# Two multiplies of the chunk loop on another engine, and a reciprocal on the other side of a broadcast, in a linear-attention block

## The reference

```
xn   = layernorm(x)
q, k, v = silu(xn @ Wq), silu(xn @ Wk), silu(xn @ Wv)         # 16 heads of 64
for each chunk of 128 tokens, per head:
    scores = (q_i @ k_i^T) * mask                             # mask = exp(-s*(i-j)), lower triangle
    o_i    = scores @ v_i + lam_q * (q_i @ kv)
    kv     = lam_c * kv + (k_i * lam_k)^T @ v_i               # 64x64 state per head
o = (o - mean(o)) * rsqrt(var(o) + 1e-5) * gamma + beta
s = (o * sigmoid(xn @ Wg1 @ Wg2)) @ Wo
g = silu(xn @ (W + lora)^T + b)
y = x + s * g
```

## Time and profile before

| | |
|---|---|
| time, median of 3 runs | 746.3 us (746.19 to 748.85) |
| profiled execution, its own time | 746.53 us |
| its span, slowest core (core 6) | 744.8 us |
| spans of the 8 cores | 736.3 to 744.8 us |
| busy share of the span | PE 68%, DVE 40%, ACT 30%, POOL 12% |
| chunk loop, 300 to 448 us | 148 us, PE clock granted 0.65 of full speed |
| stage 4c, 554 to 745 us | 191 us, PE clock 0.76 to 738 us |

### The profile page before, as it was taken

One profiled execution on the slowest core, in us unless ns is written; L12 is line 12 of the kernel. 1 busy time (PEld: TensorE's weight loads), 2 busy tenths in 40 slices (PEclk: granted clock), 3 DMA queues, 4 the chain that ended last, 5 costly groups with the idle time before them and its releaser, 6 DMA issues.

```text
span 744.8 us, 8401 instructions; the slowest of 8 cores (736.3 to 744.8 us)
## 1 busy us (share of the span) xinstructions
PE 507.5 (68%) x2644; PEld 248.3 (33%) x2678; DVE 298.8 (40%) x627; ACT 226.4 (30%) x425; POOL 89.5 (12%) x76
## 2 busy tenths in 40 slices
PE   0118181999999993456666666899976686776773
PEld 0003131444444441234444443134433232333321
DVE  1350515121021001555555556410006777787784
ACT  1134434366333331133333331652331111111110
POOL 0000000000002000244454441000000000000000
PEclk9999586899999997575575576589995868787787
DMA  8771302000058995100000002230001223143243
GB/s 250 246 227 57 113 28 85 1 1 1 0 195 174 176 177 156 51 1 1 1 1 1 1 1 68 85 114 0 1 1 28 39 47 56 29 57 57 29 57 58
DMA packets 14049, 49.73 MB, mean 67 GB/s; under 512 B 3728, under 2 KB 3729, under 8 KB 13878
## 3 DMA queue, kind: packets, MB, share of 16 engines
q0 software_dynamic: 2448, 16.78, 14.1%
q1 hardware_dynamic: 9254, 24.02, 10.5%
q10 hardware_dynamic: 2304, 8.39, 3.6%
HBM read 40.79 MB, written 16.78 MB: 77 GB/s over the span
## 4 chain that ended last, share of the span: by engine, by line
PE 46%; DVE 18%; issue 9%; ACT 9%; DMA 8%; another core or an unknown queue 7%; DVEq 1%; SPq 1%; POOL 0%; ACTq 0%; POOLq 0%
PE pb L436 15%; PE pb L830 8%; PE pb L946 6%; DMA LANDB<-wq 3%; DVE SAB L613 2%; PE pb L662 2%; PE pb L817 2%; DVE RSROW L918 2%; PE pb L538 2%; PE pb L669 2%; PE pb L649 2%; PE pb L599 2%; DMA LUPF<-lup 2%; ACT VO L691 2%
## 5 line engine op out<-in xcount | busy, mean ns | idle before, releaser
L436 PE MATMUL pb<-XNT,WS 128*128 128x512 bf16 x500 | 117.7, 395 | 17.6 <-ACT XNT L495 16.9
L436 PEld LDWEIGHTS pb<-XNT,WS 128*128 128x128 bf16 x512 | 51.3, 101 | 81.7 <-issue 27.6
L649 PE MATMUL pb<-SAB,VO 128*128 128x256 bf16 x128 | 29.5, 346 | 58.4 <-DVE SAB L619 34.7
L489 PE MATMUL pb<-IDB,XNTM 128*128 128x128 bf16 x128 | 13.6, 271 | 72.5 <-DVE XNTM L478 48.4
L402 DVE CAST WS<-LAND 128x1024 bf16<-128x1024 f32 x20 | 14.6, 729 | 118.0 <-DMA LAND<-w 55.2
L830 PE MATMUL pb<-WS,XNT 128*128 128x512 bf16 x251 | 58.4, 383 | 0.5 <-issue 0.3
L685 ACT ACTIVATE VO<-pb 64x256 bf16<-64x256 f32 x64 | 24.2, 377 | 109.6 <-PE pb L669 106.6
L538 PE MATMUL pb<-WS,XNT 128*128 128x512 bf16 x251 | 55.3, 379 | 1.9 <-DVE WS L402 1.6
L675 POOL TENSOR_TENSOR KVBD<-KVBD,LAMCB 128x512 bf16<-128x512 bf16 x32 | 36.9, 1152 | 139.2 <-DVE KVBD L701 66.4
L946 PE MATMUL pb<-WS,CCo 128*128 128x512 bf16 x122 | 44.2, 512 | 3.2 <-DVE CCo L932 1.2
L958 POOL DMA_DIRECT2D y<-SGT x16 | 13.8, 865 | 269.8 <-DVE SGT L953 269.8
(11 more groups left out here) (100 smaller groups left out, 768.4 us busy)
## 6 DMA issues: line engine op xcount, KB each, us to landing
y<-SGT POOLq DMA_DIRECT2D x16, 512.0 KB, 5.6
XV<-x ACTq DMA_DIRECT2D x12, 512.0 KB, 13.3
XTS<-x ACTq DMA_DIRECT2D x4, 512.0 KB, 8.0
LAND<-wq SPq DMA_DIRECT2D x4, 512.0 KB, 6.1
LANDB<-wq SPq DMA_DIRECT2D x4, 512.0 KB, 6.4
LAND<-wk SPq DMA_DIRECT2D x4, 512.0 KB, 4.2
LANDB<-wk SPq DMA_DIRECT2D x4, 512.0 KB, 5.0
LAND<-wv SPq DMA_DIRECT2D x4, 512.0 KB, 3.9
```

Of the source, the lines that this page charges most:

```text
L436: p.pe(lambda e, k=k, oc=oc, t4=t4, bank=bank, wten=wten: e.matmul(PB[bank][:], wten[:, k * 1024 + oc * 128:k * 1024 + (oc + 1) * 128], XN ...
L489: p.pe(lambda e, f=f, xn=xn, bank=bank: e.matmul(pbh(bank)[:, f * 128:(f + 1) * 128], xn[:, f * 128:(f + 1) * 128], IDB[:], start=(f == 0) ...
L649: p.pe(lambda e, pp=pp, c=c, ob=ob, ocol=ocol, w=w, i=i: e.matmul(PB[ob][:, ocol:ocol + 256], VO[:, c * 1024 + pp * 128:c * 1024 + (pp + 1 ...
```

## The change

Three edits. In the chunk loop the multiply into QH (L638) and the decay of the state (L675) are issued to VectorE instead of GpSimd, at the same places of the program text, with the same operands. In stage 4c the square-root row itself is broadcast by the matmul, and VectorE takes the reciprocal of the broadcast 128x128 block out of PSUM into RBI in SBUF; the eight L926 read RBI in place of PSUM.

```diff
@@ -635,7 +635,7 @@
         qsrc = A(QT, 0, c * 128, [[2048, 8], [1, 128]])
         qdst = A(QH, 0, csl * 1024, [[128, 8], [1, 128]])
         lsrc = A(LAMQB, 0, 0, [[128, 8], [1, 128]])
-        p.pool(lambda e, qsrc=qsrc, qdst=qdst, lsrc=lsrc: e.tensor_tensor(
+        p.dve(lambda e, qsrc=qsrc, qdst=qdst, lsrc=lsrc: e.tensor_tensor(
             out=qdst, in0=qsrc, in1=lsrc, op=ALU.mult),
             reads=[bQT[pp][c // 4] for pp in range(8)] + [bLAMQ],
             writes=[bQH[csl]])
@@ -672,7 +672,7 @@
-            p.pool(lambda e, csl=csl, nsl=nsl, w=w: e.tensor_tensor(
+            p.dve(lambda e, csl=csl, nsl=nsl, w=w: e.tensor_tensor(
                 out=KVBD[:, nsl * 1024 + w * 512:nsl * 1024 + (w + 1) * 512],
                 in0=KVBD[:, csl * 1024 + w * 512:csl * 1024 + (w + 1) * 512],
                 in1=LAMCB[:, w * 512:(w + 1) * 512], op=ALU.mult),
@@ -915,20 +915,20 @@
             out=VROW[:], in_=PB[sb_st][0:1, 128:256],
             func=AF.Sqrt, scale=1.0 / E, bias=EPS),
             reads=[bPB[sb_st], bEPS], writes=[bROW])
-        p.dve(lambda e: e.reciprocal(out=RSROW[:], in_=VROW[:]),
-              reads=[bROW], writes=[bROW])
         p.pe(lambda e, sb_b=sb_b: e.matmul(
-            PB[sb_b][:, 128:256], ONESF[:], RSROW[:], start=True, stop=True),
+            PB[sb_b][:, 128:256], ONESF[:], VROW[:], start=True, stop=True),
             reads=[bONESF, bROW], writes=[bPB[sb_b]])
-
+        p.dve(lambda e, sb_b=sb_b: e.reciprocal(
+            out=RBI[:], in_=PB[sb_b][:, 128:256]),
+            reads=[bPB[sb_b]], writes=[bB128])
         for pp in range(8):
             bP = bCCP[par][pp]
-            p.dve(lambda e, CCt=CCt, pp=pp, sb_b=sb_b: e.scalar_tensor_tensor(
+            p.dve(lambda e, CCt=CCt, pp=pp: e.scalar_tensor_tensor(
                 out=CCt[:, pp * 128:(pp + 1) * 128],
                 in0=CCt[:, pp * 128:(pp + 1) * 128],
                 scalar=GAMB[:, pp * 128:pp * 128 + 1],
-                in1=PB[sb_b][:, 128:256], op0=ALU.mult, op1=ALU.mult),
-                reads=[bP, bPB[sb_b], bLAMC], writes=[bP])
+                in1=RBI[:], op0=ALU.mult, op1=ALU.mult),
+                reads=[bP, bB128, bLAMC], writes=[bP])
```

## The result

The changed kernel takes 773.3 us (median), the kernel before 746.7 in the runs beside it: a ratio of 1.0362, 95% interval 1.0346 to 1.0378, or 27 us slower (the medians differ by 26.6). The direction and the place were forecast, the size was not: 765.0 us, 18.3 us slower, with a range to 773.0.

What follows compares the result with a forecast made beforehand. The chunk loop was taken as bound by a ring of waits, with no engine full. Span 744.8 + 19.5 (QH) + 0 (decay) - 0.8 (reciprocal) = 763.5, 765.2 with 1.7 around the span, 765.0 as median; range 757 to 773 us.

Steps and rivals of the forecast that it cites:

- POOL's work was free: Chunk loop: GpSimd's QH and decay multiplies run about 3 us ahead of their readers, so removing them gains nothing.
- QH starts at T + 0.60, ends at T + 1.28, and L662 starts at T + 1.42: Chunk loop, half 0: QH queues behind L631 on VectorE, lasts 0.68 us, and L662 waits for it.
- T: Chunk loop: the start of L631 on VectorE in a chunk, from which the forecast counts its times.
- I take 1.3 us for each: 15 x 1.3 = 19.5 us: Chunk loop: delay from QH on VectorE in each of 15 chunks with an L662; ends 12.6 and 20.6 us.
- discount for chunks with a high clock: Chunk loop: in 8 of 15 chunks PE's clock was high before; delay there 0.84 us if it stays high.
- the ring: Chunk loop: cycle of waits, L696/L701, masks and L631 on DVE, PE matmuls, ACT copies; mean 9.03 us per chunk.
- The upper end, 20.6: Chunk loop: largest delay worked out for QH on VectorE, 7 x 1.27 + 8 x 1.47 us, all at low clock.
- Edit 2 at nothing: Chunk loop: state's decay (L675) on VectorE is covered in both halves and costs nothing; without cover half 0's costs 6 us.
- Edit 3 at -0.8 us: Stage 4c: reciprocal behind the broadcast keeps the 1.74 us path and gains in four tiles where L953 delayed it: -0.8 us.
- single-rate multiply: Rival, chunk loop: VectorE does strided QH at one element per cycle, 1.21 us, 8 us more: 773; chance 0.07.
- cheap L926: Rival, stage 4c: L926 gets shorter with an SBUF operand, 7.5 us go: 757.5; chance 0.06.
- high clock: Rival, chunk loop: PE's clock high throughout, chunk 8.95 us against 9.03, total 744.3, not slower; chance 0.04.

Runs made afterwards that it cites:

- The three single edits: Kernel before with one edit each, ratios to it: QH multiply on VectorE 1.0317, state's decay on VectorE 0.9999, reciprocal behind the broadcast 1.0027.
- QH in the gap: All three edits, but next chunk's QH issued on VectorE behind L701 of half 0, against the kernel before: ratio 1.0036, 749.9 us.
- one more swap: Kernel before with its chunk loop reordered, plus L669's state update issued first in each half: ratio 0.9280 to the kernel before, 693.1 us.
- reordered: Kernel before with scores, masks and transposes of chunk c+1 issued behind the halves of chunk c, same engines: ratio 0.9447, 707.3 us.

## Why the prediction was right and wrong

- *What bounds the loop, and that POOL's work was free:* right. The three single edits and QH in the gap show it: the loss is the place in VectorE's queue.
- *"QH starts at T + 0.60, ends at T + 1.28, and L662 starts at T + 1.42":* right to 0.01 us.
- *"I take 1.3 us for each: 15 x 1.3 = 19.5 us":* this step failed. It measured 23.7 us, 1.6 for each. L696 of half 0 came at T + 3.05 and not at T + 2.86 (L669 ends at 369.58, T + 2.88, and L696 follows 0.17 later), since 0.85 us is what L662 adds behind a running group, and behind a wait it takes 1.01: it has no predecessor to overlap, which costs 0.16 us. The row was there: L649 x4, after a wait, took 1.01 us in the earlier trace rows, and L662 x4 directly behind it 0.85. When the change put the wait in front of L662, its first matmul became the late one. And the discount for chunks with a high clock was wrong: the ring of the changed kernel is 3.77 + 3.05 + 3.89 = 10.71 us in the usual chunk, where before the mean was 9.08 and only the slowest chunks took 9.25. L662 of half 0 ran at the low clock from its start in 13 of the 15 chunks, in 6 of them although L649 in front of the wait had run at the high one, as in the chunk shown. 1.62 is so 1.27 (worked out) + 0.18 (lost overlap) + 0.17 (the fast chunks gone). The upper end, 20.6, had the clock but not the overlap.
- *Edit 2 at nothing:* right, 0.9999.
- *Edit 3 at -0.8 us:* wrong in sign, +2.0 us. The reciprocal (0.96) and L926 (+4 ns) were nearly as taken; "ACT to PE, about the same 0.14" was not (0.25), nor was the 0.10 in front of L926 (0.17). The matmul has two semaphores to wait for after the change: VectorE's, since the bank was last read by it, and ScalarE's. Before, the reciprocal's signal stood for both. From one L914 to the next the usual tile went from 10.99 to 11.22 us, more than the tails gave back; the mean went from 11.18 to 11.29, which makes 1.7 us in 15 tiles.
- *Rivals:* single-rate multiply, cheap L926 and high clock are each refuted by a row (682 ns, 344 ns, 0.57). By an estimate from the Trainium skill's figures (VectorE: DVE Perf Modes, the TRN2 errata) L926 would have become 65 ns shorter; the trace does not agree, it became 4 ns longer.
- *The total* ended 0.3 us above the range. Its sum had two terms too low, by 4.2 and 2.8 us. The worst case worked out for the first, 20.6, stood on the row of a group that had not waited, and the second had no bound for its hand-overs.

## What to carry to other kernels

Work on an idle helper engine is free as long as its lead covers it (3 us of lead for 2.12 us of work here); the faster engine is worth nothing if the instruction then stands behind others that wait for this iteration's data. Price a moved instruction by what stands ahead of it in the queue and by the state of what stands behind it: the group behind a new wait no longer overlaps the one before it and can meet a lower clock, and its rows must be taken from a group that waited too. If a loop is a ring of waits, reorder it first: the same instructions on the same engines gave 5.5% and, with one more swap, 7.2% here, where the change of engine cost 3.2%.

## What the hardware showed unexpectedly

- A group of four 128x256 matmuls at the low clock added 0.85 us behind other matmuls, which it overlapped by 0.20 us, and took 1.01 us behind 0.85 to 2.0 us of idleness. The length of the wait made no difference: two of them took 0.58 us behind 0.36 us of idleness, 0.15 more than two of the 0.85.
- A matmul with two semaphores to wait for started 0.25 us after ScalarE's end, with one 0.14 us.
- L926 waited 0.17 us behind the reciprocal on its own engine, where L932 waits 0.10 us behind L926; why is left open.
- A VectorE reciprocal takes 0.96 us on 128x128 out of PSUM, 0.94 on 1x128 and 0.16 on 128x1: it goes by the elements along the row.
- The granted clock followed the loop's order: 0.57 with the wait in it, 0.65 before (both over 300 to 448 us), 0.94 reordered (305 to 395 us, this loop being shorter).
